# Context attention: which engine copies which fill of turned probabilities

## The reference, cut to what matters

```python
def _L1_xattn_ref(x, context, w_qkv, w_proj, b_proj):
    qkv = (x @ w_qkv.T).reshape(B, N, 3, H, D).transpose(2, 0, 3, 1, 4)
    q, k, v = (qkv[0], qkv[1], qkv[2])
    kv = context.reshape(B, N_c, 2, H, D).transpose(2, 0, 3, 1, 4)
    extra_k, extra_v = (kv[0], kv[1])
    k = jnp.concatenate([extra_k, k], axis=2)
    v = jnp.concatenate([extra_v, v], axis=2)
    attn = jnp.einsum('bhnd,bhmd->bhnm', q * scale, k).astype(jnp.float32)
    attn = jax.nn.softmax(attn, axis=-1).astype(dtype)
    out = jnp.einsum('bhnm,bhmd->bhnd', attn, v)
    out = out.transpose(0, 2, 1, 3).reshape(B, N, C)
    return out @ w_proj.T + b_proj
...
x = x + _L1_xattn_ref(_layernorm(x, axis=-1), ctx_2048, ...)
```

## Time and profile before

| | us |
|---|---|
| median of 3 runs | 2447.64 (2444.84 to 2454.57) |
| the profiled execution: its time | 2451.76 |
| the profiled execution: its span | 2450.0 |
| the context attention, first scores to last output step | 434.3 to about 770 |
| busy in the whole span: PE, PEld, DVE, ACT, POOL | 2099.8, 1561.0, 1269.5, 1010.8, 272.3 |

### The profile page before, as it was taken

The page is one execution under the profiler, slowest core; times in us unless marked ns, Lnnn a source line. Parts: engine busy times, 40 slices in busy tenths (PEclk is TensorE's granted clock), DMA queues, the critical chain, the costliest instruction groups (busy, mean ns, idle before and its releaser), DMA issues. The chain is left out here.

```text
span 2450.0 us, 38336 instructions
## 1 busy us (share of the span) xinstructions
PE 2099.8 (86%) x14693; PEld 1561.0 (64%) x14693; DVE 1269.5 (52%) x2527; ACT 1010.8 (41%) x2844; POOL 272.3 (11%) x357
## 2 busy tenths in 40 slices
PE   6779997899997599689999999969997998874884
PEld 4546765566665489656666666557876776653673
DVE  5447775688885144445545454655435554551003
ACT  3236665677774145223333232433223443331212
POOL 0100000122211534200000000031002000002004
PEclk8989999999999799799999999999999999996986
DMA  3000000121213622230000000010002000021522
GB/s 126 18 1 1 1 2 28 36 56 38 57 33 112 208 61 72 97 130 10 9 9 10 1 9 1 1 31 1 1 1 85 27 10 20 1 86 66 180 95 73
DMA packets 87873, 110.53 MB, mean 45 GB/s; under 512 B 18088, under 2 KB 71344, under 8 KB 86800
## 3 DMA queue, kind: packets, MB, share of 16 engines
q1 hardware_dynamic: 82752, 94.52, 12.6%
q0 software_dynamic: 4944, 13.57, 1.7%
HBM read 77.77 MB, written 22.95 MB: 41 GB/s over the span
## 5 line engine op out<-in xcount | busy, mean ns | idle before, releaser
L920 ACT ACTIVATE ca_prob<-bank,ca_nmax 128x512 f32<-128x512 f32 x256 | 174.0, 690 | 75.6 <-DVE ca_nmax L987 75.6
L920 ACT ACTIVATE na_prob<-bank,na_nmax 128x257 f32<-128x257 f32 x256 | 118.0, 474 | 206.6 <-DVE na_nmax L987 206.6
L987 DVE TENSOR_REDUCE ca_nmax<-bank 128x1 f32<-128x512 f32 x256 | 164.2, 684 | 42.6 <-PE bank L774 42.6
L788 PE MATMUL bank<-cst,ca_prob 128*128 128x128 f32 x1024 | 141.3, 279 | 6.9 <-DVE ca_pT L993 5.2
L788 PEld LDWEIGHTS bank<-cst,ca_prob 128*128 128x128 f32 x1024 | 111.7, 142 | 53.5 <-issue 45.5
L920 ACT ACTIVATE ra_prob<-bank,ra_nmax 128x256 f32<-128x256 f32 x256 | 118.1, 481 | 64.5 <-DVE ra_nmax L987 64.5
L987 DVE TENSOR_REDUCE na_nmax<-bank 128x1 f32<-128x257 f32 x256 | 90.8, 417 | 82.6 <-PE bank L774 82.6
L2142 PE MATMUL bank<-sf_h,sf_W 128*128 128x512 f32 x512 | 120.4, 395 | 0.3 <-DVE sf_h L2214 0.3
L2036 PE MATMUL bank<-na_Wkv,na_cxT 128*128 128x512 f32 x256 | 115.4, 595 | 0.0
L2142 PEld LDWEIGHTS bank<-sf_h,sf_W 128*128 128x128 f32 x512 | 95.8, 187 | 24.3 <-DVE sf_h L2214 1.0
L987 DVE TENSOR_REDUCE ra_nmax<-bank 128x2 f32<-128x512 f32 x128 | 82.1, 684 | 38.5 <-PE bank L774 38.5
(11 more groups left out here) (464 smaller groups left out, 4630.5 us busy)
## 6 DMA issues: line engine op xcount, KB each, us to landing
xl_w<-in_L_ffn_w SPq DMA_DIRECT2D x16, 1024.0 KB, 7.5
rf_sent<-rf_w SPq DMA_DIRECT2D x13, 390.0 KB, 6.3
rf_xin<-rf_sent SPq DMA_DIRECT2D x39, 128.0 KB
dp_cx<-in_ctx_tok SPq DMA_DIRECT2D x4, 1024.0 KB, 14.8
ca_v<-in_ctx_values SPq DMA_DIRECT2D x8, 512.0 KB, 4.5
rf_W<-in_L_ffn_w SPq DMA_DIRECT2D x8, 512.0 KB
rf_rows<-rf_back SPq DMA_DIRECT2D x8, 512.0 KB
na_Wkv<-in_L_xattn_Wkv SPq DMA_DIRECT2D x1, 4096.0 KB, 16.2
```

Source lines behind the costliest of these rows:

```text
L788: mm = pe.transpose(TB[f % 2][:, j * P:(j + 1) * P], prob[:, n % 2, u, c0:c0 + P], ident)
L920: e = act.activation(prob[:, n % 2, u, hh * keys:(hh + 1) * keys], S[u][:, hh * keys:(hh + 1) * keys], ACT.Exp, bias=nmax[:, n % 2, u, hh: ...
L987: v.tensor_reduce(nmax[:, n % 2, u], S[u][:, 0:W].rearrange("p (h k) -> p h k", h=per), AX.X, ALU.max, negate=True).then_inc(maxed, 1)
```

## The change

With `copy_late` set, which only the context attention does, VectorE copies fills 0 and 1 of a round and ScalarE fills 2 and 3. The orders on both engines follow: VectorE takes max 2 before copy 0 and puts copy 1 behind max 3; ScalarE does its four exponentials in one go and then copies fills 2 and 3. Fills 2 and 3 are now turned after waits on VectorE's copies of fills 0 and 1 of the same round, and fills 0 and 1 after waits on ScalarE's copies of fills 2 and 3 of the round before. The number of copies on each engine, two a round, stays, and so does the order of TensorE's instructions.

```diff
@@ turn(n, f), TensorE
-                if fill >= 2:
+                if copy_late and fill >= 2:
+
+                    if f >= 2:
+                        pe.wait_ge(copied_v, 2 * n + f - 1)
+                    else:
+                        pe.wait_ge(copied_a, 2 * n - 1 + f)
+                elif fill >= 2:
                     pe.wait_ge(copied_v if f % 2 == 0 else copied_a, (fill - 2) // 2 + 1)
@@ ScalarE's loop
-                    if 1 <= n <= NR:
+                    if 1 <= n <= NR and not copy_late:
                         copy_turned(n - 1, 1)
                     if n < NR:
                         exps(n, 2)
...
                     if 1 <= n <= NR:
+                        if copy_late:
+                            copy_turned(n - 1, 2)
                         copy_turned(n - 1, 3)
@@ VectorE's loop
                 for use in slots[n][0]:
                     shared(use)
+                if copy_late and n < NR:
+                    maxima(n, 2)
                 if 1 <= n <= NR:
                     copy_turned(n - 1, 0)
                 if FILLS == 4:
                     if n < NR:
-                        maxima(n, 2)
+                        if not copy_late:
+                            maxima(n, 2)
                         maxima(n, 3)
+                    if copy_late and 1 <= n <= NR:
+                        copy_turned(n - 1, 1)
                     if not values_due(n):
                         for use in slots[n][1]:
                             shared(use)
-                    if 1 <= n <= NR:
+                    if 1 <= n <= NR and not copy_late:
                         copy_turned(n - 1, 2)
@@ context_attention_layer
-                         stack=stack)
+                         stack=stack, copy_late=True)
```

More of the change, by code:

```diff
@@ L561, in attention_stream @@
                      stack=None,
-                     divide=False, made=lambda b, k: False, place=None, late=()):
+                     divide=False, made=lambda b, k: False, place=None, late=(), copy_late=False):
     nc = g.nc
```

## The result

| | before | after |
|---|---|---|
| median of 16 runs each | 2445.93 us (2439.16 to 2456.46) | 2466.41 us (2455.93 to 2478.2) |
| ratio after / before | | 1.0081, 95% interval 1.0064 to 1.0098 |
| time of the profiled execution (span) | 2451.76 (2450.0) | 2456.85 (2455.1) |
| context attention, first scores to last turn | 327.0 | 347.2 |
| everything behind it, code untouched | 1688.7 | 1673.8 |

The account below looks back on a forecast made before the run. It took a ring through several engines (scores, maximum, exponentials, next scores) to bound the kernel; 48 x 0.24, 7 x 0.57 and 7 x 0.26 sum to +17 us, hence 2466 us, range 2457 to 2475.

Parts of the forecast that it names:

- What goes: Copy 1 leaves ScalarE's queue, but exp 3 still needs VectorE's max 3; only 0.07 of 0.47 us a round gained.
- What comes: Copy 1 becomes VectorE's sixth step at +3.74, ending +4.42, so TensorE starts turning fill 3 at +4.54.
- From fill 3 to the scores: On TensorE the next scores start 0.55 us after fill 3's matmuls start, as behind the spread, at +5.12.
- Rival B: Scores' weight loads run ahead behind fill 3 on TensorE, the shorter bound: +12.9 us, 2462; chance 0.15.
- The size in plain rounds: Fill 3 sets the period of the 48 plain rounds, each 0.24 us longer than 4.88.
- r = 1: Round where the spread, then the scores, follow fill 3 without slack; longer by fill 3's delay, +0.57 us.
- r = 2: Round whose max 0 starts late, at +1.42; period 5.81 in place of 5.55, +0.26 us.
- What is hidden: ScalarE's late copies 2 and 3 end before fill 1 of the next round; copy 3 shows only from 0.8 us lateness.
- The sum: Over 62 rounds: 11.5 plain, 4.0 and 1.8 in the two special kinds, tail left out; +17 us (17.3).
- The base: Time of the kernel before onto which the change was added: middle of four times near 2449.5 us, giving 2466.
- A: Rival: only the ring through ScalarE's exponentials counts, so removing copy 1 gives -29 us, 2420; chance 0.08 (0.03 for all).
- C: Rival: ScalarE's late copies hold fills 0 and 1 of the next round; +26 us, 2475; chance 0.05.

Follow-up runs that it names:

- e3: Kernel after, with the next round's scores ahead of fill 3 in TensorE's queue in all rounds but r = 1; layer 338.4 us, ratio 1.0048.
- e2: Kernel after, but VectorE takes all four maxima first, then copy 0 and copy 1; plain period still 5.15 us, ratio 1.0078.
- e5: Kernel after, with copy 1 made twice on VectorE, first into a tile nobody reads; plain period 5.75 us, layer 388.5, ratio 1.0250.
- e4: Kernel after, with copy 1 ahead of max 3 on VectorE; plain period 5.37 us, layer 361.3, ratio 1.0130.
- e6: Kernel after, with copy 3 made twice on ScalarE, first into a spare tile; plain period 5.15 us, ratio 1.0080.
- e1: Kernel before, with only max 2 moved ahead of copy 0 on VectorE; layer 327.0 us, ratio 1.0001.
- e8: Kernel before, with the spread ahead of fill 3 at r = 1 on TensorE and its copy ahead on ScalarE; layer 324.4 us, ratio 0.9981.
- e9: From e8: ScalarE copies fills 0 and 3, copy 0 ahead of exp 0; VectorE takes four maxima, then copies fills 1 and 2; 2439.29 us, ratio 0.9965.
- e7: Kernel after, with the spread ahead of fill 3 at r = 1 on TensorE and its copy ahead on ScalarE; ratio 1.0060.

## Why the prediction was right

By its own steps:

- *What goes: 0.07 at most.* Right. Exp 3 starts at +3.88 (predicted +3.87), 0.72 after max 3. e3's even rounds of 4.83 show the leg itself (predicted 4.81), and e2 the stronger form: while fill 3 holds the scores, even 0.38 more gives nothing.
- *What comes: copy 1 as sixth step, fill 3 at +4.54.* Right: 589.91 is +3.76, the loads +4.56. e5 shows that the chain has no slack, e4 that the same step under max 3 costs more.
- *From fill 3 to the scores: 0.55.* 590.74 to 591.30 is 0.56. Rival B, 0.47, falls: the scores' loads didn't run ahead but started 0.17 after the last turn's, in 55 rounds. The Trainium skill's "TensorEngine Tiling (Array Packing)", Key Properties, says that a change of tiling mode drains TensorE. The trace agrees: there is that gap of 0.17 where the shape changes, and none between the loads of fills 0 and 1 and those of the projection behind them, which have one shape. The Trainium skill's "TensorE: Matmul & The Clock Gate", Step-by-step, has weight loads pulled ahead where the row groups don't conflict. Transposes over all 128 rows don't meet that condition, and no load is seen to run ahead at this place.
- *The size in plain rounds.* This is the mis-sized term: 0.27 for 0.24. Max 0 starts 0.76 after scores that follow turns directly (586.15 to 586.91), not 0.73 as after scores that had waited; that 0.03, with 0.56 for 0.55, makes 0.76 + 3.00 + 0.68 + 0.12 + 0.03 + 0.56 = 5.15.
- *r = 1:* 6.04 - 5.47 = 0.57, as predicted. *r = 2:* 5.79 - 5.54 = 0.25 for 0.26.
- *What is hidden.* Right: copy 3 may be 0.49 later (e6) without showing in plain rounds, within the 0.8 that I counted (0.25 + 0.57). Only at r = 2 does 0.08 of it show.
- *The sum.* 48 x 0.27 + 7 x 0.57 + 7 x 0.25 = 18.7 for 17.3, of 20.2 measured in the layer. The layer's further 1.5 is 0.9 in two rounds of the last batch at a lower clock (5.29 and 5.94 in place of 5.15) and 0.5 in the tail behind the last scores, which I had put at 0.2 at most.
- *The base.* I put the change on 2449; the kernel before has its median at 2445.9. That 2466 hit the median of 2466.41 to half a us is luck: the base was 3 too high and the difference 3 too small.

Of the rivals, A is refuted by e2, B by the rows after, C by e6 for this change; but C's mechanism is real, since e3 calls it up as soon as fill 3 itself is moved back.

## What to carry to other kernels

When work is moved from one engine's queue to another's, count the steps in the queue it enters up to each thing that is awaited, and look at what stands behind that thing in the waiting engine's queue: the scores never needed fill 3, but they couldn't pass it. Taking a copy out of a ring is worth only the slack to the next leg, here 0.05 to 0.07 of 0.47 us. And read a change by the length of its own stage: of one profiled execution each, the totals showed a quarter of what the layer and the medians showed.

## What the runs showed of the hardware

**The clock.** Windows of the last batch after (columns as in the earlier trace rows):

```profile
756.00:762.00 6.00, 3.42 (x29) 2.40 (x28) 4.02 (x7) 4.83 (x13) 0.00 (x0) 1.00 0.00 0
762.00:768.00 6.00, 6.00 (x58) 3.77 (x57) 3.68 (x6) 3.74 (x11) 0.00 (x0) 0.72 0.01 3
...
762.00:764.00 2.00, 2.00 (x14) 1.03 (x13) 0.41 (x1) 0.79 (x2) 0.00 (x0) 0.50 0.00 0
```

TensorE was busy 3.42 of 6 us, and the granted clock then stood at 0.72 in the mean of the next 6 us; from 762 to 764 it was 0.50, the lower of its two levels (1.2 GHz of 2.4). The two rounds from 757.05 to 768.28 took 5.29 and 5.94 in place of 5.15, 0.9 more. The last batch has no projections for a next one, so TensorE stands idle longest there. The periods in that batch of before, e1, e3, e8 and e9 are those of the others; after, e2, e4, e5, e6 and e7, all with fill 3 or max 3 held by a sixth or seventh step, lost 0.9 to 3 us in its rounds. Whether the longer waits cause that wasn't isolated.

**Steps and rows.** Maxima and copies of 128 x 512 on VectorE have rows of 0.68 us but follow each other at 0.60, and ScalarE's copies, 0.60 in their rows, at 0.47 to 0.49. All sums above are made with the step; with the row, five steps would put a plain round 0.4 above the 5.15 measured.

**Untouched stages.** Behind the layer the same code took 1673.8 to 1688.7 us in the eleven profiled executions (one of each kernel), a spread of three quarters of the effect studied.
